# A four-layer attention and mixture-of-experts kernel: a longer ring of row tiles, a reordered turning of tiles, store waits moved into the list part, and shorter integer rounding

## The reference, cut to what matters

```
x = x + attn_a(layernorm(x))     # 16 causal heads of 16 dims, then Wo
x = x + ffn(layernorm(x))        # experts
x = x + attn_b(layernorm(x))     # softmax over 1024 keys, one head of 256, w_fc, second layernorm
x = x + ffn(layernorm(x))        # experts

def ffn(x):
    t = x * rsqrt(mean(x * x) + EPS) * norm_scale
    logits = t @ gate_w + gate_b                 # 8 experts, the best 2 of each token
    top_v, top_i = top_k(logits, 2); probs = softmax(top_v)
    return x + sum over the 2: probs * (swiglu(t @ w1[e] + b1[e]) @ w2[e] + b2[e])
```

## Time and profile before

| what | value |
|---|---|
| median of 3 runs | 1760.12 us (1759.5 to 1762.02) |
| the profiled execution's own time | 1772.88 us |
| its span, first to last instruction | 1771.1 us |
| PE busy | 1643.6 us (93%) |
| DVE, ACT, POOL busy | 1278.3, 1048.5, 796.2 us |
| mean granted PE clock | 0.945 |
| HBM read and written | 74.21 and 56.69 MB |

### The profile page before, as it was taken

One profiled execution on the slowest core, in us unless ns is written; L12 is line 12 of the kernel. 1 busy time (PEld: TensorE's weight loads), 2 busy tenths in 40 slices (PEclk: granted clock), 3 DMA queues, 4 the chain that ended last, 5 costly groups with the idle time before them and its releaser, 6 DMA issues. The chain is left out here.

```text
span 1771.1 us, 35927 instructions
## 1 busy us (share of the span) xinstructions
PE 1643.6 (93%) x11154; PEld 1205.8 (68%) x11155; DVE 1278.3 (72%) x2671; ACT 1048.5 (59%) x1853; POOL 796.2 (45%) x779
## 2 busy tenths in 40 slices
PE   9889999999998894999999998799965999999998
PEld 4444444444442673999999997344534999999997
DVE  5688888888881666777777776368886777777776
ACT  4437767677676443666666664556654666666664
POOL 4541111111112122666666665225542666666664
PEclk9999999999998875999999999899975999999999
DMA  5654445254431752332222222301112222223232
GB/s 164 181 149 116 115 107 133 87 137 114 109 97 43 170 185 84 67 47 48 47 47 47 48 47 36 110 0 48 48 48 85 42 48 47 47 47 48 47 47 39
DMA packets 102684, 140.85 MB, mean 80 GB/s; under 512 B 18177, under 2 KB 86785, under 8 KB 99521
## 3 DMA queue, kind: packets, MB, share of 16 engines
q1 hardware_dynamic: 65382, 90.62, 19.5%
q0 software_dynamic: 31808, 37.32, 13.2%
q10 hardware_dynamic: 5402, 11.80, 1.9%
HBM read 74.21 MB, written 56.69 MB: 74 GB/s over the span
## 5 line engine op out<-in xcount | busy, mean ns | idle before, releaser
L596 ACT ACTIVATE a_Pt<-a_p_st 128x512 f32<-128x512 f32 (+2 forms) x624 | 302.5, 594 | 134.3 <-PE a_p_st L677 133.9
L623 DVE TENSOR_REDUCE mx<-a_p_sn 128x2 f32<-128x256 f32 (+1 forms) x600 | 333.7, 629 | 62.8 <-PE a_p_sn L660 52.7
L1362 ACT COPY R<-values_then_w 128x1024 f32 x284 | 283.0, 1044 | 38.9 <-issue 21.5
L1311 PE MATMUL e_p_g<-e_tT,R 128*128 128x128 f32 x2272 | 280.6, 277 | 1.6 <-ACT e_tT L1354 1.6
L1311 PE MATMUL e_p_l<-e_tT,R 128*128 128x128 f32 x2272 | 278.3, 276 | 0.0
L1323 PE MATMUL e_p_y<-w,e_hid 128*128 x1136 | 268.9, 380 | 5.8 <-DVE e_hid L1431 5.8
L1311 PEld LDWEIGHTS e_p_g<-e_tT,R 128*128 128x128 f32 x2272 | 268.3, 194 | 2.5 <-ACT e_tT L1354 2.4
L1311 PEld LDWEIGHTS e_p_l<-e_tT,R 128*128 128x128 f32 x2272 | 266.9, 193 | 0.1
L573 POOL TENSOR_SCALAR_AFFINE_SELECT a_Pt<-a_Pt 128x512 f32<-128x512 f32 x128 | 81.2, 635 | 366.1 <-ACT a_Pt L596 366.1
L1323 PEld LDWEIGHTS e_p_y<-w,e_hid 128*128 128x128 f32 x1136 | 205.0, 190 | 28.1 <-issue 6.2
L660 PE MATMUL a_p_sn<-Kst,Qst 96*128 96x128 bf16 (+1 forms) x720 | 220.9, 333 | 1.9 <-PEq L161 1.8
(11 more groups left out here) (224 smaller groups left out, 2396.2 us busy)
## 6 DMA issues: line engine op xcount, KB each, us to landing
qk_parts<-a_part SPq DMA_DIRECT2D x64, 192.0 KB, 3.1
a_Vst<-values_then_w SPq DMA_DIRECT2D x16, 512.0 KB, 18.3
o_rows<-a_OT ACTq DMA_DIRECT2D x32, 256.0 KB, 2.7
values_then_w<-in_mlp SPq DMA_DIRECT2D x16, 512.0 KB, 4.2
t_rows<-R SPq DMA_DIRECT2D x16, 512.0 KB, 3.0
Kst<-qk_parts SPq DMA_DIRECT2D x14, 384.0 KB
Qst<-qk_parts SPq DMA_DIRECT2D x14, 384.0 KB
a_Ot<-o_rows SPq DMA_DIRECT2D x64, 64.0 KB
```

The lines of the kernel that those rows point to most:

```text
L596: act.activation(weights(kb, slice(h, h + n), a, b), p_st[:, i % RING, 0:n * (b - a)].rearrange("p (n w) -> p n w", n=n), ACT.Exp, scale=D ...
L623: dve.tensor_reduce(mx[:, hs[0]:hs[-1] + 1, place], p_sn[:, (s + k) % RING, 0:w * len(hs)].rearrange("p (h w) -> p h w", w=w), AX.X, ALU.m ...
L1311: mm = pe.matmul(bank[:, s, c * P:(c + 1) * P], copied[:, s, k, at:at + P], tT[:, s, k * P:(k + 1) * P], start=(k == 0), stop=(k == KD - 1))
L1362: act.copy(copied[:, s, :, cols], g["w1"][:, bass.ds(e, 1), :, cols].rearrange("p a k n -> p (a k) n")).then_inc(copied_done, 1)
```

## The change

The change does six things.

1. In `out_rows` the ring of t is 24 tiles in slots 8 to 31 (T_GROUPS = 6 groups, six semaphores): `scaled(j)` waits only from j = 24 on, for the first store of its slot.
2. The waits for the stores of t and x leave the end of `out_rows`. In the first `rank` SP waits for them at its end, and POOL waits for those of t ahead of its first gather. The wait for the last half's stores of `attend_a` goes to SP in `out_rows`, ahead of the load of pair 12; that half's OT is then the tile xs, which lives through the program.
3. The first load of Ot is split: SP issues three heads, ACT the sums and the fourth head.
4. On ACT the last four `normal` stand in a row at step 35, ahead of `turned(26)`.
5. In `rank` (both times) the rounding of the counts and of the slots takes one chained step less each, with one scaling more near the end.
6. In `layer_b` items 0 and 1 are both halves of the dims of the first half of the tiles, items 2 and 3 those of the second.

```diff
-    OT = mem.sb("OT", [P, 2, 512])
+    OT = [mem.sb("OT", [P, 512])[:, :], g["xs"][:, :, :].rearrange("p s d -> p (s d)")]
...
-            for c in range(2):
-                act.wait_ge(o_out[c], 16 * U)
+            act.wait_ge(o_out[0], 16 * U)
...
+T_GROUPS = 6
...
     def t_of(j):
-        return g["R"][:, 8 + j % 8, :]
+        return g["R"][:, 8 + j % (T_GROUPS * GROUP), :]
...
+                if q == NT // 2 - QB // 2:
+                    sp.wait_ge(g["last_out"], 16 * U)
+                load_values(sp, q, range(HG))
+                load_sums(sp, q)
...
-            load(0)
+            load_values(sp, 0, (0, 1, 2))
...
-            for s in range(2):
-                sp.wait_ge(t_out[s], 16 * (NT // 8))
-            sp.wait_ge(x_out, 16 * (NT // GROUP + 1))
...
+            load_sums(act, 0)
+            load_values(act, 0, (3,))
             for j in range(STEPS):
+                if j - 7 == NT - GROUP:
+                    for i in range(GROUP):
+                        normal(j - 7 + i)
...
-                if 0 <= j - 7 < NT:
+                if 0 <= j - 7 < NT - GROUP:
                     normal(j - 7)
...
-                if j >= 8:
-                    dve.wait_ge(tp_done, j - 7)
-                    dve.wait_ge(t_out[j // GROUP % 2], 16 * (j // 8))
+                if j >= T_GROUPS * GROUP:
+                    dve.wait_ge(tp_done, j - T_GROUPS * GROUP + 1)
+                    dve.wait_ge(t_out[j // GROUP % T_GROUPS], 16)
...
             sp.wait_ge(b_in, 16)
+            for stored, count in x_stores + t_stores:
+                sp.wait_ge(stored, count)
             sp.wait_ge(w_out, 16)
...
-            link(dve.tensor_scalar(cnt[:, 0, :], cnt[:, 0, :], 1.0 / P, 0.5 - 0.5 / P, ALU.mult, ALU.add))
-            link(dve.tensor_scalar(cnt[:, 0, :], cnt[:, 0, :], ROUND, None, ALU.add))
-            link(dve.tensor_scalar(cnt[:, 1, :], cnt[:, 0, :], ROUND, None, ALU.subtract))
+            link(dve.tensor_scalar(cnt[:, 0, :], cnt[:, 0, :], 0.5 * (P - 1), ROUND * P, ALU.add, ALU.add))
+            link(dve.tensor_scalar(cnt[:, 1, :], cnt[:, 0, :], ROUND * P, None, ALU.subtract))
+            dve.tensor_tensor(cnt[:, 3, :], cnt[:, 1, :], upto[:, 0:E], ALU.add).then_inc(chain, 1)
+            count[0] += 1
...
-            link(dve.tensor_scalar(whole_tile[:, :], slot[:, :], 1.0 / P, 0.5 / P - 0.5, ALU.mult, ALU.add))
-            link(dve.tensor_scalar(whole_tile[:, :], whole_tile[:, :], ROUND, None, ALU.add))
-            link(dve.tensor_scalar(whole_tile[:, :], whole_tile[:, :], ROUND, None, ALU.subtract))
+            link(dve.tensor_scalar(whole_tile[:, :], slot[:, :], -0.5 * (P - 1), ROUND * P, ALU.add, ALU.add))
+            link(dve.tensor_scalar(whole_tile[:, :], whole_tile[:, :], ROUND * P, None, ALU.subtract))
...
+            link(dve.tensor_scalar(cnt[:, 0, :], cnt[:, 2, :], 1.0 / P, None, ALU.mult))
...
+            for stored, count in t_stores:
+                pool.wait_ge(stored, count)
             pool.wait_ge(token_done, 1)
...
             def turned(b, i):
-                k, half = i // 2, i % 2
+                half, k = i // 2, i % 2
...
             def turn(b, i):
-                k, half = i // 2, i % 2
+                half, k = i // 2, i % 2
```

More of the change, by code:

```diff
@@ L498, in attend_a @@
     o_copied = [mem.sem(f"o_c{c}") for c in range(2)]
-    o_out = [mem.sem(f"o_out{c}") for c in range(2)]
+    o_out = [mem.sem("o_out0"), g["last_out"]]
     def is_first(u):
@@ L769, in out_rows @@
         mem.sem(s) for s in ("st_d", "mv_d", "root_d", "inv_d", "coef_d"))
-    n_done, t_done, added, tp_done, tT_done, l_done, x_out = (
-        mem.sem(s) for s in ("n_d", "t_d", "added", "tp_d", "tT_d", "l_d", "x_out"))
-    t_out = [mem.sem(f"t_out{s}") for s in range(2)]
+    n_done, t_done, added, tp_done, tT_done, l_done = (
+        mem.sem(s) for s in ("n_d", "t_d", "added", "tp_d", "tT_d", "l_d"))
+    t_out, x_out = g["t_out"], g["x_out"]
     STEPS = NT + 10
@@ L778, in t_of, with turned_rows_of, load_values, load_sums @@
     def t_of(j):
-        return g["R"][:, 8 + j % 8, :]
+        return g["R"][:, 8 + j % (T_GROUPS * GROUP), :]
     def x_of(j):
         return g["X"][:, j, :]
+    def turned_rows_of(q):
+        b, at = 2 * q // QB, 2 * q % QB * P
+        return o_dram[b * HG:(b + 1) * HG, :, at:at + 2 * P].rearrange("u (h c) t -> h c u t", c=PAD)
+    def load_values(eng, q, heads):
+        for h in heads:
+            eng.dma_start(Ot[DK * h:DK * (h + 1), q % DEEP], turned_rows_of(q)[h, 0:DK]).then_inc(o_in[q % DEEP], 16)
+    def load_sums(eng, q):
+        eng.dma_start(Ot[DK * HG:C * HG, q % DEEP], turned_rows_of(q)[:, DK]).then_inc(o_in[q % DEEP], 16)
     with nc.Block(no_gpsimd_drain=True) as block:
@@ L804, in store @@
                 sp.dma_start(t_dram[rows, :].rearrange("(t p) d -> p t d", p=P),
-                             g["R"][:, 8 + GROUP * (c % 2):8 + GROUP * (c % 2 + 1), :]).then_inc(t_out[c % 2], 16)
+                             g["R"][:, 8 + GROUP * (c % T_GROUPS):8 + GROUP * (c % T_GROUPS + 1), :]
+                             ).then_inc(t_out[c % T_GROUPS], 16)
                 sp.wait_ge(added, GROUP * (c + 1))
@@ L823, in _ @@
             sp.dma_start(acc[T:T + P, :], g["X"][:, 0, :]).then_inc(x_out, 16)
-            for s in range(2):
-                sp.wait_ge(t_out[s], 16 * (NT // 8))
-            sp.wait_ge(x_out, 16 * (NT // GROUP + 1))
+            stores_of_rows = [(t_out[s], 16 * len(range(s, NT // GROUP, T_GROUPS))) for s in range(T_GROUPS)]
+            g["stores"] = stores_of_rows, [(x_out, 16 * (NT // GROUP + 1))]
         @block.tensor
@@ L998, in _, with rank @@
                 pool.tensor_tensor(x_of(j), x_of(j), n_of(j), ALU.add).then_inc(added, 1)
-def rank(nc, mem, g, t_dram, w_dram):
+def rank(nc, mem, g, t_dram, w_dram, t_stores, x_stores):
     Q = 2 * NT
@@ L2118, in program @@
         g["w1"] = g["VW"][:, :, :].rearrange("p (e k) n -> p e k n", k=KD)
+        g["xs"] = keep.sb("xs", [P, 2, D])
+        g["t_out"] = [keep.sem(f"t_out{s}") for s in range(T_GROUPS)]
+        g["x_out"] = keep.sem("x_out")
+        g["last_out"] = keep.sem("last_out")
         g["w_in"] = keep.sem("w_in")
@@ L2146, in program @@
         g["R"] = keep.sb("R", [P, NT, D])
-        g["xs"] = keep.sb("xs", [P, 2, D])
         g["w2"] = keep.sb("w2", [P, E, KI, D])
@@ L2153, in program @@
             phase(out_rows, "a3_", o_dram, t_dram, x_dram)
-            phase(rank, "r1_", t_dram, w_dram)
+            phase(rank, "r1_", t_dram, w_dram, *g["stores"])
         phase(experts, "e1_", t_dram, w_dram, x_dram, spent, True)
@@ L2160, in program @@
             phase(layer_b, "b_", x_dram, t_dram, out)
-            phase(rank, "r2_", t_dram, w_dram)
+            phase(rank, "r2_", t_dram, w_dram, [], [])
         phase(experts, "e2_", t_dram, w_dram, out, [], False)
```

15 lines of the change are left out of this document (6 added, 9 removed).

## The result

The changed kernel takes 1747.06 us (median of 5 runs, 1742.15 to 1748.61); the kernel before, beside it, 1759.5 us (5 runs, 1756.97 to 1762.02). The ratio is 0.9931, with a 95% interval of 0.9915 to 0.9946. The forecast was 1749. The profiled execution of the changed kernel took 1746.57 us itself and lies among its other runs, so nothing suggests that profiling adds time: the 1772.88 of before was a slower execution.

A forecast was written before the change was run, and what follows sets the result against it. PE, busy 93% of the span, was taken as the bound, so only stretches where something else ends last could move. Ring 1.0 plus the other terms 10.0 made 11.0 us off 1760.1: forecast 1749, range 1735 to 1756.

The forecast's parts named there:

- The likeliest case: Whole kernel: timed runs of before hold neither the 2.64 us wait nor its slow-clock stretch; 11.0 us gained, 1749, chance 0.47.
- hand-over from `attend_a`: Start of `out_rows`: loads start 1.7 us earlier, splitting the first load gives 0.8; together 2.5 us, bounds 1.5 to 2.8.
- ring, without a spell: `out_rows`: only DVE's two short waits for stores of t leave, 1.0 us; with the slow-clock stretch 12.8.
- store waits moved: End of `out_rows`: `rank` starts 0.5 us after PE's last logits, at 672.5 not 675.2; 2.7 us, low bound 2.0.
- normalisations in a row: End of `out_rows`: last t 1.6 us earlier, but PE's logits queue behind; 0.7 us taken, bounds -0.5 to 2.0.
- rounding, two lists: `rank`, both times: fewer chained steps, one added scaling; net 0.3 us a list, 0.6 in all, bounds 0.2 to 0.9.
- turning by tile halves: `layer_b`: PE's waits of 1.33, 0.88 and 0.89 us go, plus 0.8 at the start; 3.9 discounted to 3.5, bounds 1.5 to 5.5.
- the profiled spell: `out_rows`, profile of before: PE's clock at 0.50 from 636 to 656 after DVE's 2.64 us wait, costing 9.1 us.
- The rival that all timed runs have the spell (1737): `out_rows`: timed runs also hold the slow-clock stretch, so 22.8 us are gained from 1760.1: 1737, chance 0.27.
- The premise that all have it or none has: Timed runs of before lie within 2.5 us of each other, so the slow-clock stretch is in all or none.
- My estimate from the rule: `out_rows`: going by the page alone, the slow clock would end after a tile or two, 3.5 us; ring then worth 7.
- the backlog on PE that the prediction named: End of `out_rows`: six tiles of logits and four turnings behind four normalisations, 6 us at 0.86 a tile, ending at 672.

The follow-up runs named there:

- the second profile of before: The kernel before, unchanged, profiled a second time: 1760.91 us.
- the experiment's 15.02: The changed kernel with the last four normalisations spread over the steps as before: 1745.42 us (one run).
- The ring alone: The kernel before with only the ring of 24 tiles and its six semaphores: 1752.61 us (12 runs), ratio 0.9953.
- the short ring: The changed kernel with the ring of t back at 8 tiles: 1750.26 us (12 runs), ratio 0.9953.
- Both forced stalls: The changed kernel plus one DVE wait in `out_rows`: ahead of tile 15, 4.68 us stall, 1753.92 us; ahead of tile 21, 7.91 us stall, 1755.76 us.
- the one of the unsplit load: The changed kernel with all five issues of the first pair's load on SP, none on ACT: 1747.86 us (one run).

## Why the prediction came out right

The time, 1747.06, lies 2 us from the forecast and in the range. The likeliest case was the nearest to what happened, but three of its terms were off (the hand-over, the ring and the row), the cost of the first gather was missing, and these errors partly cancelled: that the number came out so close is in part luck. Against the second profile of before, in us:

| step | forecast | measured |
|---|---|---|
| hand-over from `attend_a` | 2.5 | 1.5 |
| ring, without a spell | 1.0 | 3.0 to 3.3 |
| store waits moved | 2.7 | 2.7 |
| normalisations in a row | 0.7 | -0.4 |
| rounding, two lists | 0.6 | 0.7 |
| turning by tile halves | 3.5 | 4.2 |
| first gather (at nothing in the prediction) | 0 | -1.5 to -2.2 |
| sum | 11.0 | 9.5 to 10.5 |

The measured values come from the table of stages (6.38 - 4.90; 64.70 - 61.70 and 64.70 - 61.36; 3.24 - 0.57; 14.97 - 15.42 and the experiment's 15.02 - 15.42; 25.00 - 24.65 twice; 3.7 between the scores and 0.5 ahead of them, the mean of ten profiles with the new order, 26.1, against 26.6 of four with the old; 5.10 - 7.33, and 5.10 - 6.55 in the profile with the smallest loss). The 0.5 ahead of the scores is not shown: the ten lie at 25.6 to 26.6, the four at 25.9 to 27.0. The timed difference is 12.4 us. The 1.9 to 2.9 left may be executions of before with a longer stall or more time at the lower clock, or stages that no edit touches; which, is not shown.

**Hand-over.** The block's end came as forecast, 1.7 us earlier, but the issues that follow take longer so close behind the stores: 0.5 us of it is lost there, and the split gives 0.33 and not 0.8. I had scaled 1.75 us for four issues down to 1.3 for three; they took 2.00. Nor is the length of the issues all of it: in the nine other profiles with the split three took 1.76 to 2.02 us, and PE started 4.83 to 5.14 us behind the last store, no sooner where they were short. What PE waits for is the landing, which the sum took to move with the issues.

**Ring.** To take the profiled spell as an exception held in part: a second profile of before has waits of 1.3 us, no fall of the clock, and stands at the timed median. The rival that all timed runs have the spell (1737) falls with it. The premise that all have it or none has fell too: it rested on three runs within 2.5 us, and the 54 runs of before beside the experiments range from 1751.91 to 1775.08. But I counted only the two short waits. Between tiles 10 and 31 the second profile takes 44.31 us, the changed kernel 41.93, so 2.4 us left with 1.3 us of waits, and what the other 1.1 were is not shown; the rest of the 3.3 came at the start of the phase, where the clock was at 0.50 until about 586 in the one, 9.8 us after PE's first turning, and until about 581 in the other, 7.5 us after it. That the spells are rare is not shown either. The ring alone gave 8.3 us in timed runs, at least 5.5, where the forecast had 1.0 and stages without a spell give 3.0; its higher mean clock fits that the rest is less time at the lower level. And 3 of 12 runs with the short ring were 4.8 us or more above the other nine, at lower mean clocks. Some timed executions of before probably have a spell; how many can't be read from a time or from a mean clock.

**Does the stall cause the spell?** Both forced stalls, 4.68 and 7.91 us, were followed by the lower clock. In the eleven other profiles taken after the prediction, none of which has such a stall, the clock is 1.00 from 586.1 at the latest to the drain. So a stall of this size brings the fall. PE itself idled 7.65 us in the one and 4.66 in the other. In before it idled 2.38 us (631.7 to 634.1), and the clock fell at 636.0. In the eleven its longest gap in that stretch is 1.25 us, and nothing fell. In the drain, though, the clock falls after gaps of 1.14 and 0.94 us. No run repeats a gap near 2.4 us, so that the stall of 2.64 brought the spell of before is argued from larger ones and not shown. The spell's length is not explained: 2.3 us lost behind a stall of 4.68, 4.2 behind one of 7.91, 9.1 behind one of 2.64. Waits of 1.3 us in three pieces and 2.9 in four had none. My estimate from the rule that idleness throttles and activity releases (the Trainium skill, "TensorE: Matmul & The Clock Gate", Part 1, The HAM clock gate), that a spell would be over after a tile or two, fits the short stall, where the clock was back at 627.85, about 4 us after PE's return; it does not fit or the long stall, where PE was booked in full for about 20 and 10.5 us at 0.50.

**Store waits and the row.** The 2.7 us came, but the two edits are one gain and not two. With the row and the waits both in place the hand-over takes 1.06 us (sum of the two stages 16.5, where it was 18.2); with the waits moved and no row it is 0.49 (15.5); with both moved 0.57 (16.0). The row would have been worth 1.7 us had the waits stayed. With them gone nobody waits for the last t, and the backlog on PE that the prediction named (turnings and six tiles of logits behind four normalisations, at clock 0.50) is what is left: 0.4 us lost, near its bound of -0.5. The mistake was to lean on PE's idle gap of 3 us; the clock falls in that gap, and the backlog is then worked off at the lower level, 0.86 us a tile.

**Turning.** The three waits were nearly all of it: 3.55 of the 3.7 us between the scores; the 0.5 at the start is not clear of the scatter. So 3.9 was worked out and 3.7 to 4.2 measured, and the discount that I took for DVE and ACT was not needed.

**The first gather.** I costed the six waits on POOL at nothing, because the stores land long before. The stores do; the waits still cost. They stand between POOL and an instruction that is itself on the path, and 0.6 us there brought the gather close enough to SP's loads to lose 1.2 to 2.0 more. The prediction said of a moved wait what is queued behind it, but looked only at when it is met, not at what it costs when it has been met long ago, nor at which transfers the shift runs into.

## What to carry to other kernels

A wait moved off the path should go to an engine whose next instruction isn't awaited: six waits that had long been met cost 0.6 us in front of a gather, and the loads that the gather then met cost 1.2 to 2.0 more; the same waits on DVE cost 0.13. Two edits that hide the same landing are not two gains: measure each in the presence of the other, as here one of them turned into a small loss. Where one profile is slower than the timed runs, take a second profile before a spell in it is taken for the rule, and look at the mean granted clock of the timed runs, which is there for each.

## What the runs showed of the hardware

- PE's clock fell from 1.00 to 0.50 in both forced stalls (4.68 and 7.91 us of DVE), and came back some 4 and 10.5 us after PE was booked in full again. In every profile it falls in the drain of `out_rows`; in the one of the unsplit load it fell only at 647.1, 9.8 us behind `inverse_sums(31)` and not 7.6 as in the changed kernel, and the stage to the last logits took 14.60 us in place of 15.4.
- Semaphore waits that were met long before held up POOL's indirect DMA by 0.6 us (0.53 to 1.15 after `token`), and DVE by 0.13 us.
- A gather of 128 rows reached PE 3.1 us after its start when it started 1.4 us or more ahead of eight broadcast loads, and 4.3 to 5.1 us after it when it started 0.7 us ahead (eight profiles).
- SP's issues of four loads of 64 KB took 2.25 us right behind the stores (one run) and 1.75 to 1.79 after the stores' landing (three); three beside ACT's two took 1.76 to 2.02 (ten).
